# A decoder of thirteen sublayers on one core: weight waits inside the norms, the first loads in pieces, the Mamba preparation spread over the engines

## What is computed

```python
L0_attn   # 16 heads of 64, causal
L0_xattn, L0_ffn          # rotary retention with ctx; 8-bit product
L1_attn   # Mamba, forward and backward scans, both summed
L1_xattn, L1_ffn          # 16 heads of 8 with a mask; integer weights
L2_attn, L2_xattn, L2_ffn # gated linear attention; distance mask; 8 experts
L3_attn, L3_xattn
L3_ffn    # two layers of local attention and GEGLU
# in L1_attn, per direction (softplus over 256 channels, 16 states):
delta = jax.nn.softplus(delta @ dt_proj_w.T + dt_proj_b)
y = _selective_scan(x, delta, A, B, C, D, reverse=reverse)   # ends in y + u * D
# in L1_ffn:
w = (q.astype(jnp.float32) - 128.0).reshape(K // g, g, N) * scales[:, None, :]
```

## Time and profile before

| | |
|---|---|
| median of 3 runs | 1672.06 us (1669.94 to 1674.89) |
| the profiled execution | 1672.33 us, span 1670.6 us |
| busy in the span | PE 1232.4, DVE 998.1, ACT 879.2, POOL 499.5 us |
| 0 to 15.3 us | no matmul until 15.29 |
| dtproj of L1_attn | 274.2 to 285.0 us |
| block L1_attn_dt | 285.3 to 320.3 us, DVE busy 34.3 |
| the scans of L1_attn | 321 to 592 us |
| longest pack transfer | 2,824 KB in 13.7 us |

### The profile page before, as it was taken

The page is one execution under the profiler, slowest core; times in us unless marked ns, Lnnn a source line. Parts: engine busy times, 40 slices in busy tenths (PEclk is TensorE's granted clock), DMA queues, the critical chain, the costliest instruction groups (busy, mean ns, idle before and its releaser), DMA issues. The chain is left out here.

```text
span 1670.6 us, 21147 instructions
## 1 busy us (share of the span) xinstructions
PE 1232.4 (74%) x6968; PEld 617.4 (37%) x6976; DVE 998.1 (60%) x2025; ACT 879.2 (53%) x1809; POOL 499.5 (30%) x583
## 2 busy tenths in 40 slices
PE   6999655166666677967646986976957979878886
PEld 2575331022222223532212553432424434633462
DVE  2574445999999936712756644444544738737752
ACT  2574232599999925844123772242632645733653
POOL 0363001288888823100222210001201214513440
PEclk9999876589999987988877997986887989999998
DMA  3000000000000016011005300005113310000000
GB/s 141 1 2 1 21 8 0 0 1 0 1 0 1 0 64 140 7 45 38 0 0 158 77 2 17 0 23 101 39 53 78 75 53 0 2 0 1 0 2 13
DMA packets 42908, 48.75 MB, mean 29 GB/s; under 512 B 2992, under 2 KB 39984, under 8 KB 41520
## 3 DMA queue, kind: packets, MB, share of 16 engines
q1 hardware_dynamic: 42800, 47.40, 10.7%
HBM read 34.28 MB, written 13.11 MB: 28 GB/s over the span
## 5 line engine op out<-in xcount | busy, mean ns | idle before, releaser
L1357 POOL TENSOR_TENSOR L_attn_z<-L_attn_state,L_attn_r 128x1024 f32<-128x1024 f32 x64 | 150.9, 2359 | 40.0 <-DVE L_attn_state L1343 33.7
L1343 DVE TENSOR_TENSOR_SCAN L_attn_state<-bank,L_attn_w 128x512 f32<-128x512 f32 x128 | 149.0, 1206 | 0.0
L1254 PE MATMUL bank<-L_attn_z,const 128*128 128x512 f32 x256 | 138.5, 669 | 1.9 <-POOL L_attn_z L1361 1.4
L807 DVE CUSTOM_DVE_ANT_0 L_xattn_core_logits<-bank,L_xattn_mask 128x256 f32<-128x256 f32 x256 | 98.6, 422 | 54.6 <-PE bank L590 42.2
L1238 PE MATMUL bank<-L_attn_rows,L_attn_select 128*128 128x512 bf16 x90 | 34.0, 433 | 88.7 <-ACT L_attn_C L1306 45.8
L1294 ACT ACTIVATE L_attn_r<-L_attn_after_dt,L_attn_half_guard,L_attn_A 128x512 f32<-128x512 f32 x128 | 96.5, 802 | 0.0
L1284 ACT ACTIVATE bank<-L_attn_dt,L_attn_A 128x510 f32<-128x510 f32 x128 | 86.5, 676 | 13.1 <-DVE L_attn_state L1343 13.1
L719 ACT ACTIVATE L_xattn_core_probs<-bank 128x512 f32<-128x512 f32 x132 | 71.5, 596 | 37.6 <-PE bank L633 26.7
L590 PE MATMUL bank<-L_xattn_core_rows 48*128 48x256 bf16 x384 | 64.7, 313 | 31.4 <-DMA L_xattn_core_rows<-L_xattn_core_slots 17.6
L1361 POOL TENSOR_TENSOR L_attn_z<-L_attn_z,L_attn_C 128x1024 f32<-128x1024 f32 x32 | 75.8, 2368 | 23.6 <-ACT L_attn_C L1306 23.6
L1324 DVE TENSOR_TENSOR L_attn_w<-bank,L_attn_udt 128x1024 f32<-128x1024 f32 x64 | 78.2, 1222 | 5.6 <-remote 1.2
(11 more groups left out here) (477 smaller groups left out, 2993.8 us busy)
## 6 DMA issues: line engine op xcount, KB each, us to landing
L_xattn_core_rows<-L_xattn_core_slots SPq DMA_DIRECT2D x24, 384.0 KB, 5.9
weights<-in_pack_L_ffn SPq DMA_DIRECT2D x2, 2118.5 KB, 8.2
L_xattn_core_slots<-L_xattn_core_k_parts SPq DMA_DIRECT2D x24, 128.0 KB, 2.0
L_attn_core_rows<-L_attn_core_slots SPq DMA_DIRECT2D x8, 384.0 KB, 5.7
weights<-in_pack_L_ffn SPq DMA_DIRECT2D x1, 2824.0 KB, 13.7
weights<-in_pack_L_attn SPq DMA_DIRECT2D x1, 2304.0 KB, 8.5
L_xattn_core_slots<-L_xattn_core_q_parts SPq DMA_DIRECT2D x12, 192.0 KB, 2.2
weights<-in_pack_L_xattn SPq DMA_DIRECT2D x1, 1539.5 KB, 6.6
```

Source lines behind the costliest of these rows:

```text
L807: last = nc.vector.tensor_tensor_reduce(logits[:, c], scores_bank[side][:, c * S:(c + 1) * S], mask[:, 2 * b + c, :], 1.0, MASKED, ALU.add ...
L1254: last = nc.tensor.matmul(y_bank[2 * c + half][:], ident, z[:, g % NS, c], start=False, stop=False, skip_group_check=True)
L1343: nc.vector.tensor_tensor_scan(state[:, g % NS, c, ::step], a_bank[c][:, ::step], w[:, g % 2, c, ::step], 0.0, ALU.mult, ALU.add).then_inc ...
L1357: nc.gpsimd.tensor_tensor(z[:, g % NS], state[:, g % NS], r[:, g % NS], ALU.mult).then_inc(z_done, 1)
```

## The change

- `weights_in` and `weights_wait` are gone. `fetch_next` issues the next pack from SyncE inside the sublayer's first working block, `next_arrived` waits for it inside `add_and_norm` (before L3_ffn1, inside the last `add_to_x`).
- The first loads come as six pieces and a rest, with a semaphore for each piece; jobs 0, 4 and 16 of the first `stream` wait for what they need. wq and wk are interleaved in the pack. The two casts run on POOL in that stream.
- In L1_attn the skip term becomes eight matmuls with ident scaled by D, the forward `part_rows` goes to POOL during dtproj, the backward one to POOL in L1_attn_dt; ACT works by quarters with one table set; POOL multiplies the backward udt.
- L1_ffn's integers ride in its pack and are widened inside the norm. L2_attn's gate product goes by halves into `add_and_norm`; `sym` and `near` of L2_xattn into its stream (job 0 waits for `sym`); L3_ffn0's copy to ACT in the shift's block; the result is written by halves inside the last norm.

```diff
@@ Core
-    def prefetch(self, sp, i):
-        if i < len(self.stages):
-            g = self.stages[i]
-            sp.dma_start(self.arena[i % 2][:, 0:self.width(g)], self.dram["pack_" + g]).then_inc(self.loaded, 16)
+    def fetch_next(self, sp):
+        i = self.stages.index(self.group)
+        if i == 0:
+            sp.dma_start(self.ctx[:], self.dram["ctx"]).then_inc(self.late_in, 16)
+        if i + 1 < len(self.stages):
+            g = self.stages[i + 1]
+            sp.dma_start(self.arena[(i + 1) % 2][:, 0:self.width(g)], self.dram["pack_" + g]).then_inc(self.loaded, 16)
+    def next_arrived(self, sp):
+        i = self.stages.index(self.group)
+        if i == 0:
+            sp.wait_ge(self.late_in, 16)
+        if i + 1 < len(self.stages):
+            sp.wait_ge(self.loaded, 16 * (i + 2))
@@ weights_wait and weights_in are removed
@@ stream, in PE's part
+                for ready, value in needs.get(j, ()) if needs else ():
+                    pe.wait_ge(ready, value)
@@ add_and_norm
+                if inputs:
+                    pe.wait_ge(inputs_ready, h + 1)
...
+            for h in range(2 if inputs else 0):
+                inputs(h).then_inc(inputs_ready, 1)
...
-                nc.vector.tensor_tensor(xh[h], K.bank[2 + h][:], inv_std[:, h], ALU.mult)
+                nc.vector.tensor_tensor(xh[h], K.bank[2 + h][:], inv_std[:, h], ALU.mult).then_inc(normalised, 1)
+        @block.sync
+        def _(sp):
+            K.next_arrived(sp)
+            for h in range(2 if result is not None else 0):
+                sp.wait_ge(normalised, h + 1)
+                sp.dma_start(halves(result)[h], xh[h]).then_inc(K.result_out, 16)
+            if result is not None:
+                sp.wait_ge(K.result_out, 32)
@@ L0_attn
-    weights_in(K, "L0_attn")
+    K.use_weights("L0_attn")
+    def arrive(sp):
+        for n, dst, src in (("first_tokens", x[:, 0:HALF], K.dram["x"][:, 0:HALF]),
+                            ("first_wqk", arena[:, 0:first], pack[:, 0:first]),
+                            ("last_wqk", arena[:, first:last], pack[:, first:last]),
+                            ("last_tokens", x[:, HALF:T], K.dram["x"][:, HALF:T]),
+                            ("wv", arena[:, last:wv_end], pack[:, last:wv_end]),
+                            ("const", K.const[:], K.dram["pack_const"])):
+            sp.dma_start(dst, src).then_inc(arrived[n], 16)
+        sp.dma_start(arena[:, wv_end:K.width("L0_attn")], pack[:, wv_end:]).then_inc(K.loaded, 16)
+        sp.wait_ge(K.loaded, 16)
+        K.fetch_next(sp)
...
-            stream(K, "L0_attn_qkv", jobs)
+            wait_for = {j: [(arrived[n], 16) for n in names] for j, names in (
+                (0, ("first_tokens", "first_wqk")), (4, ("last_wqk",)), (2 * NG, ("last_tokens", "wv")))}
+            stream(K, "L0_attn_qkv", jobs, on_sync=arrive, on_pool=narrow, needs=wait_for)
@@ L1_attn, first convolution, ACT
+                            for side in range(2):
+                                for c in range(DC):
+                                    nc.scalar.activation(skip[:, side, c], ident, ACT.Copy,
+                                                         scale=W(f"D{side}")[:, c:c + 1])
@@ L1_attn, dtproj stream
-                for d in range(2) for c in range(DC) for h in range(2)])
+                for d in range(2) for c in range(DC) for h in range(2)],
+                act_last=lambda act: nc.scalar.preload_act_table_set(LN_EXP), on_pool=lambda pool: part_rows(pool, 0))
@@ L1_attn, block L1_attn_dt
-                        chain.link(nc.scalar.activation(soft[d][:], dt[d][:], ACT.Abs))
-                        chain.link(nc.scalar.activation(soft[d][:], soft[d][:], ACT.Exp, scale=-1.0))
                         for c in range(DC):
+                            chain.link(nc.scalar.activation(soft[d][:, c], dt[d][:, c], ACT.Abs))
+                            chain.link(nc.scalar.activation(soft[d][:, c], soft[d][:, c], ACT.Exp, scale=-1.0))
                             nc.scalar.activation(soft[d][:, c], soft[d][:, c], ACT.Ln, bias=1.0).then_inc(soft_done, 1)
...
-                    for c in range(DC):
-                        chain.link(nc.vector.tensor_scalar(conv[:, c], u[0][:, c], W("D0")[:, c:c + 1], None, ALU.mult))
-                        nc.vector.scalar_tensor_tensor(out=conv[:, c], in0=u[1][:, c], scalar=W("D1")[:, c:c + 1],
-                                                       in1=conv[:, c], op0=ALU.mult, op1=ALU.add).then_inc(added, 1)
-                    part_rows(nc.vector, chain, 1)
...
-                            nc.vector.tensor_tensor(udt[d][:, c], u[d][:, c], dt[d][:, c], ALU.mult)
+                            if d == 0:
+                                nc.vector.tensor_tensor(udt[d][:, c], u[d][:, c], dt[d][:, c], ALU.mult)
...
-                    part_rows(nc.gpsimd, Chain(pool, parted), 0)
-                    pool.wait_ge(backward_parted, 1)
+                    part_rows(pool, 1)
                     nc.gpsimd.tensor_copy(batches(mirrored[0:96, :]), batches(rows[1][0:96, :])[:, :, ::-1])
+                    for c in range(DC):
+                        pool.wait_ge(dt_ready, DC + c + 1)
+                        nc.gpsimd.tensor_tensor(udt[1][:, c], u[1][:, c], dt[1][:, c], ALU.mult)
...
-                        pe.wait_ge(added, c + 1)
                         for h in range(2):
-                            nc.tensor.matmul(K.bank[4 + 2 * c + h][:], ident, conv[:, c, h * HALF:(h + 1) * HALF],
-                                             start=True, stop=False, skip_group_check=True)
+                            for side in range(2):
+                                nc.tensor.matmul(K.bank[4 + 2 * c + h][:], skip[:, side, c],
+                                                 u[side][:, c, h * HALF:(h + 1) * HALF],
+                                                 start=(side == 0), stop=False, skip_group_check=True)
@@ L1_ffn
-                sp.dma_start(w1q[:], K.dram["fc1_q"]).then_inc(in_, 16)
-                sp.dma_start(w2q[:], K.dram["fc2_q"]).then_inc(in_, 16)
...
+        def widen(dve):
+            nc.vector.tensor_scalar(w1[:], W("fc1_q").bitcast(I32), 128.0, None, ALU.subtract)
+            nc.vector.scalar_tensor_tensor(out=w2[:], in0=W("fc2_q").bitcast(I32), scalar=128.0, in1=W("fc2_scales"),
+                                           op0=ALU.subtract, op1=ALU.mult)
+
-        norm_core(K, "L1_ffn_pre", x, n, W("ln_gamma"), W("ln_beta"))
+        norm_core(K, "L1_ffn_pre", x, n, W("ln_gamma"), W("ln_beta"), dve_first=widen, on_sync=K.fetch_next)
@@ L2_xattn
-        with nc.Block() as block:
-            @block.scalar
-            def _(act):
-                nc.scalar.activation(near[:], W("localization_length"), ACT.Exp, scale=-1.0).then_inc(near_done, 1)
...
-                nc.vector.tensor_scalar(sym[:], W("odd"), W("wsym"), None, ALU.mult)
...
         def make_masks(dve):
+            nc.vector.tensor_scalar(sym[:], W("odd"), W("wsym"), None, ALU.mult).then_inc(sym_done, 1)
...
-               dve_first=make_masks)
+               dve_first=make_masks, act_first=distance_slope, on_sync=fetch, needs={0: [(sym_done, 1)]})
@@ L2_attn
-                nc.vector.tensor_tensor(o[:], o[:], outgate[:], ALU.mult)
-        add_and_norm(K, "L2_attn_norm", lambda h: [(W("wout"), halves(o)[h])])
+        add_and_norm(K, "L2_attn_norm", lambda h: [(W("wout"), halves(o)[h])],
+                     inputs=lambda h: nc.vector.tensor_tensor(halves(o)[h], halves(o)[h], halves(outgate)[h], ALU.mult))
@@ L3_ffn
-                nc.vector.tensor_copy(K.x0[:], x[:])
+        keep_x = (lambda act: nc.scalar.activation(K.x0[:], x[:], ACT.Copy)) if layer == 0 else None
+        shift_tokens(K, tag + "_shift", shifted, on_act=keep_x, on_sync=K.fetch_next)
```

221 lines of the change are left out of this document (108 added, 113 removed).

## The result

The changed kernel took 1622.78 us in the median of its first four runs (1618.78 to 1631.27) against 1671.0 (1666.37 to 1674.89): a ratio of 0.9718 [0.9692, 0.9744], 47 us faster. The profiled execution took 1626.72 us (span 1624.9), 45.6 less than the profiled one of before.

A forecast was written before the change was run, and what follows sets the result against it. No engine bounds the whole span; a serial program of stages ending in all-engine barriers does. Start 10.9, boundaries 18.3, Mamba 5.1 and end 0.7 sum to 35.0 us off 1672.3: 1637.3, predicted median 1637.0, range 1627 to 1643.

The forecast's parts named there:

- Start: At the kernel's head, the first product waits for 256 KB of x and 256 KB of weights only: 10.9 us gained.
- they land together: Rival on the first loads: all pieces arrive with the last byte, gaining 2.2 us instead of 10.9, 1645.7 us; chance 0.11.
- The 2 us of setup a transfer: First loads: if each of seven pieces paid full setup, the second would land near 6 us, giving 9.3 us.
- Boundaries: Between stages, fewer barriers and waits ahead of the next product: 18.3 us in all, 5.2 of it at seven plain ones.
- norm's barrier waited for a pack: Sign of a wrong forecast: the weight wait moved into the norm was to cost nothing, packs having landed earlier.
- Mamba: Block L1_attn_dt, with work taken off DVE and partly given to POOL: 5.1 us gained, between 2 and 10.
- The turns: In L1_attn_dt, DVE and POOL alternate when both work out of SBUF, stretching DVE's operations; the block gives 5.1 us.
- without it 13.7: Rival for L1_attn_dt: DVE is not held up by POOL, gaining 13.7 us instead of 5.1, 1628.4 us; chance 0.22.
- End: Writing the result in halves inside the last norm: 0.7 us gained at most, taken in full.
- The attention cores: Sign of a wrong forecast: these stages, left alone by the change, change length by more than 3 us in all.
- a fall of the clock behind 2.82 us of idle time: Row at a stage's start, used against PE keeping its upper clock: it fell behind idle time as short as the new gaps.
- PE keeps its clock: Rival: shorter idle ahead of eight stages keeps the upper clock, up to 1.8 us each, 14.4 in all, 1622.6; chance 0.08.

The follow-up runs named there:

- the first repeat: The changed kernel run again unaltered, beside the kernel before: median 1627.25 us (1616.18 to 1631.2), ratio 0.9723.
- the runs on the gaps: Added norm product (changed kernel 1636.11 us, kernel before 1675.73); unread PE products (1615.08, 1656.65); seven plain boundaries' weight waits inside norms alone, kernel before (1657.03).

## Why the prediction was off

- **Start**: 10.9 forecast, 10.9 measured. The pieces arrived in order; that they land together did not happen. The 2 us of setup a transfer, which the prediction takes from the Trainium skill's "SBUF — State Buffer" (they stand in its part on the DMA setup-cost knee, ahead of the one named), were not paid twice: the second piece was there 3.2 us behind its issue.
- **Boundaries**: 18.3 forecast, 18.6 in the trace (5.4 + 8.3 + 1.9 + 1.5 + 0.4 + 1.1). L2_ffn gave 1.02 instead of 0.75. No norm's barrier waited for a pack.
- **Mamba**: 5.1 forecast, 5.9 measured. The turns came at the A operations, at the first quarter and at the scans, but only three of the four A operations waited (1.78, 1.05 and 1.06 us; the fourth took 0.18), so A was done 5.9 us behind the block's start and not 8.1. The first quarter began 5.9 us behind the block's start (271.77), where the forecast had it wait for POOL's mirror copy and begin 9.1 behind it. It met POOL's last subtraction and the copy instead, and its two first operations took 3.04 and 1.94 us for 1.20 and 1.23: 2.5 of the 3.2 were paid after all. The backward quarters took 5.7, forecast 5.5. The Trainium skill's rule of full blocking ("SBUF — State Buffer", practical consequences under the shared port) holds for this block: with it 5, without it 13.7, measured 5.9.
- **End**: 0.7 forecast, 0.6 measured.
- **The attention cores**, whose change by over 3 us was to be a sign of being wrong, took 673.5 us in both profiled executions (first to last instruction on their tiles, summed), but 668.8 in the trace of the first repeat. Of these 4.7 us 3.1 are in L3_attn, which had 10 us less at the lower level there: the sign would have fired for the clock, and not for the change.
- **The step that failed** is one that the sum did not contain: it counted each shortened gap at its own length and PE's clock behind it at nothing. The forecast rested on a single row, a fall of the clock behind 2.82 us of idle time, and read it as a rule: as short a gap loses the clock, so it is lost everywhere. Gaps of 2.88 us in the changed kernel end at 0.50 in some places and at 1.00 in others, and differently from run to run: of the 69 gaps of 2.8 to 2.9 us in all traces, 27 led into a first microsecond at 0.50 and 26 into one at 1.00. The rival "PE keeps its clock" named the mechanism, gave up to 14.4 us and 1622.6, and had 0.08; the measured surplus over the 36.0 of the terms is 11. Its chance should have been several times that, and the range should have reached to it.

L0_ffn, from norm to norm, shows the size on one stage; the row of the changed kernel stands first, then that of the version with udt on VectorE, which has the same code in this stage:

```profile
189.13:220.66 31.53, 17.40 (x74) 14.02 (x74) 11.30 (x22) 7.28 (x11) 0.00 (x0) 0.68 0.08 26
```

```profile
188.40:216.21 27.81, 13.67 (x74) 10.50 (x74) 11.32 (x21) 7.27 (x11) 0.00 (x0) 0.88 0.09 30
```

Same work, 3.7 us apart by the clock alone. The kernel before took 30.64 there, at 0.72: in this stage the changed kernel's profiled execution was the slower one, in spite of a boundary shorter by 0.7. In L3_attn it was the other way round, 124.3 us against 127.1. Over all fourteen traces L3_attn took 121.2 to 121.5 us in the four with the least time at the lower level (37.6 us) and 126.8 to 127.5 in the three with the most (54.6).

Where the surplus lies can be read for the profiled pair, whose difference of 45.6 us is 9.6 above the terms. From norm to norm, and less the terms, L1_attn gave 5.0, L3_xattn 2.0, L1_ffn 1.0, L2_attn 0.9 and L1_xattn 0.4: the five sublayers that began at a higher clock than before hold 9.2. L3_attn, which began at 0.98 and at 1.00, gave 2.1, and the rest together lost 1.7. So the heads of the sublayers are not all of it; PE's gaps inside a stage fall differently too.

What stays open: how the 11 us of the medians divide between the norms and the inside of the stages; the division above is that of one pair of executions. The mean time at the lower level is 435 us in the kernel before and 393 in the changed one; at 0.30 us each the 42 us would be some 12.6, but part of them is idle time that is gone (the L1_ffn hole) and cost nothing. No run held the clock equal in both kernels, so the 11 are the difference between a median and a sum of rows, with the runs on the gaps as support for their cause.

## What to carry to other kernels

Where stages are short and a wait of some 3 us lies between them, cost a shortened gap twice: its own length, and the work behind it at both clock levels; put the second as a full branch into the range, since one row can't tell whether a gap of that length keeps the clock. Here the clock was kept behind each of 27 gaps of up to 2.2 us and behind none of 20 from 4.8 us on, and went either way between. Unread products in such a gap are a cheap test of what the clock is worth before anything is rebuilt. When work moves to POOL, move it beside VectorE operations that read PSUM or beside VectorE's waits; beside its scans over SBUF three quarters of it were paid here (2.1 us of a product of 2.78).

## What was unexpected

- Single executions of the changed program differ by 15 us (1616.2 to 1631.2), largely in the order of the granted clock. The kernel before, where nearly every gap lost the clock, spread by 6 and 5 us in two of three sets (1668.1 to 1674.0, 1670.3 to 1675.0), and by 12 in the third, of 17 runs (1662.4 to 1674.7).
- A VectorE operation on 128x32 elements took 1.05 to 1.78 us beside POOL and 0.18 without, so small operations are the worst to put there.
- ACT loads its table (1.28 us) again at the head of L1_attn_dt, at 271.77, though it had loaded the same set at 260.17 in dtproj's block; taking the second request out removed it.
- Three blocks that kept their own wait got longer by 0.3 to 0.7 us when the norms ahead of them took over the wait for the weights. Why was not tried.
